# Second attention rebuilt: 32-row tiles for two heads at a time, one ring of three bank pairs, rows spread by DMA

## The reference, cut to what matters

```
q = rope((x @ wq)) -> 32 heads of 8      k = rope((x @ wk)) -> 8 heads of 8      v = (x @ wv) -> 8 heads of 8
scores = einsum('bhqd,bhkd->bhqk', q, repeat(k, 4)) / 8 ** 0.5        # 1024 x 1024, causal
probs  = softmax(where(causal, scores, -inf))
out    = einsum('bhqk,bhkd->bhqd', probs, repeat(v, 4)) -> (2, 1024, 256) @ wo
```

## Time and profile before

| | |
|---|---|
| median of three runs | 2036.06 us |
| the profiled execution's own time | 2036.67 us |
| its span, first to last instruction | 2034.0 us |
| second attention, from the first selection matmul (1169.17) to the end of the last division (1816.9) | 647.7 us |
| its 16 units, counted from one output copy of ACT to the next | 37.5 us for the first, 542.6 for the next 14, 31.2 for the last |

### The profile page before, as it was taken

How to read it: one execution, slowest core, us unless ns; L and a number is a source line. 1 busy time by engine, 2 the same in 40 slices (tenths; PEclk the granted TensorE clock), 3 DMA queues, 4 the chain that set the end, 5 groups by cost and what they waited for, 6 DMA issues and landing times. The chain is left out here.

```text
span 2034.0 us, 46207 instructions
## 1 busy us (share of the span) xinstructions
PE 1759.8 (87%) x15316; PEld 1102.3 (54%) x15316; DVE 1459.2 (72%) x3038; ACT 1157.2 (57%) x2198; POOL 559.5 (28%) x486
## 2 busy tenths in 40 slices
PE   3899999999999999997284789989989999973897
PEld 1577777777777777775142324444444444432455
DVE  4577777777777777776755587778788878825574
ACT  4566666666666666664565325555555555555453
POOL 1555545555545555541311500000000000002011
PEclk9999999999999999999597879999999999986899
DMA  4212211112211111210001000000000000001000
GB/s 127 83 46 50 49 44 47 42 42 49 49 38 47 43 41 47 49 40 3 0 1 64 1 1 1 2 1 0 0 0 0 0 0 0 1 1 62 1 21 21
DMA packets 47508, 56.67 MB, mean 28 GB/s; under 512 B 8337, under 2 KB 29010, under 8 KB 47442
## 3 DMA queue, kind: packets, MB, share of 16 engines
q1 hardware_dynamic: 47442, 55.82, 10.6%
HBM read 20.15 MB, written 2.10 MB: 11 GB/s over the span
## 5 line engine op out<-in xcount | busy, mean ns | idle before, releaser
L1622 ACT ACTIVATE a_prob<-psum 128x768 f32<-128x768 f32 (+5 forms) x384 | 303.7, 810 | 270.3 <-PE psum L1588 146.4
L1658 DVE TENSOR_REDUCE a_mx<-psum 128x1 f32<-128x512 f32 (+3 forms) x608 | 380.7, 659 | 78.0 <-PE psum L1530 48.9
L224 POOL TENSOR_TENSOR x<-x,y (+1 forms) x64 | 54.4, 880 | 980.1 <-ACT y L196 980.1
L1527 PE MATMUL psum<-a_kd,a_qp 128*128 128x512 f16 (+3 forms) x768 | 242.8, 340 | 36.5 <-DVE a_mx L1658 30.0
L1553 PE MATMUL psum<-a_qf,a_kd 128*128 128x512 f16 (+3 forms) x768 | 209.2, 327 | 4.0 <-ACT a_prob L1622 4.0
L528 POOL TENSOR_TENSOR a_swp<-a_swp,a_sin 128x512 f32<-128x512 f32 x128 | 163.4, 1276 | 162.8 <-DMA a_swp<-a_lin 157.9
L1527 PEld LDWEIGHTS psum<-a_kd,a_qp 128*128 128x128 f16 x768 | 73.9, 97 | 226.5 <-DVE a_mx L1658 176.0
L884 DVE TENSOR_REDUCE a_nmax<-psum 128x1 f32<-128x1024 f32 (+7 forms) x256 | 190.8, 746 | 0.6 <-PE psum L599 0.6
L532 POOL TENSOR_TENSOR a_rope<-a_swp,a_cosd 128x512 f32<-128x512 f32 x128 | 164.1, 1282 | 12.4 <-POOL a_swp L528 4.8
L879 DVE TENSOR_TENSOR a_pt_lo_big<-psum,a_pt_hi_big 128x512 f16<-128x512 f32 (+3 forms) x256 | 138.5, 581 | 30.8 <-ACT a_pt_hi_big L751 30.1
L756 ACT ACTIVATE a_prob_big<-psum,a_nmax 128x1024 f32<-128x1024 f32 (+3 forms) x128 | 121.7, 951 | 67.9 <-DVE a_nmax L884 64.6
(11 more groups left out here) (264 smaller groups left out, 4737.4 us busy)
## 6 DMA issues: line engine op xcount, KB each, us to landing
a_swp<-a_lin SPq DMA_DIRECT2D x256, 128.0 KB, 2.3
x<-_attn_hidden_states_dram SPq DMA_DIRECT2D x4, 512.0 KB, 5.5
a_w_raw<-in_L_attn_Wq_dram SPq DMA_DIRECT2D x16, 128.0 KB, 2.2
a_w_raw<-in_L_attn_Wk_dram SPq DMA_DIRECT2D x16, 128.0 KB, 2.3
a_w_raw<-in_L_attn_Wv_dram SPq DMA_DIRECT2D x16, 128.0 KB, 2.2
a_wo_raw<-in_L_attn_Wo_dram SPq DMA_DIRECT2D x1, 2048.0 KB
out_dram<-x SPq DMA_DIRECT2D x4, 512.0 KB, 2.9
f_raw<-in_L_ffn_w_dram SPq DMA_DIRECT2D x2, 704.0 KB, 5.1
```

The lines of the kernel that those rows point to most:

```text
L1527: last = pe.matmul(work(slot, i * n, i * n + n), qp[:, wb, t * P:(t + 1) * P], kd[:, wb, j0 + i, a:e], start=True, stop=not edge)
L1622: act.activation(dst, src, ACT.Exp, scale=SCALE).then_inc(prob_ready, 1)
L1658: dve.tensor_reduce(mx[:, t, j0:j0 + per, p0], work(slot, 0, per * n).rearrange("p (j n) -> p j n", j=per), AX.X, ALU.max).then_inc(work_f ...
```

## The change

What it does:

1. **32-row tiles.** `qp`, `qf` and `kp` hold four heads in four blocks of 32 rows, as before, but no block-diagonal `kd` is made. A QK or KQ matmul now contracts over the 32 rows of one head. Two heads are issued behind one another into the two banks of a pair, each in its own 32 rows of the array.
2. **Rows spread by DMA.** Instead of selection matmuls and copies, SP issues 24 DMAs for each unit (8 rows of 1024 f16 each, L1480 and L1481) that put the rows of queries and keys into place, up to three units ahead. The row that subtracts the maximum is written into `kp` once, ahead of the projections (one `tensor_scalar` over 3 x 1024 columns).
3. **One ring.** All work of a unit, 24 QK jobs (S), 24 KQ jobs (X), 2 turns of maxima (M) and 2 of outputs (O), goes through a ring of three bank pairs in one fixed order, `JOBS`. Job k may start on PE when the reader of job k-3 is done: DVE for S, M and O, ACT for X.
4. **Larger scans.** One DVE instruction takes the maxima of two heads: 24 in place of 38 for each unit.
5. **The causal edge of KQ** is no longer a matmul: GpSimd zeroes it in `prob` after the exponent (`affine_select`, 16 for each unit), and the context waits for it. The mask matmuls of QK stay.
6. **Smaller pieces.** `prob` is two rings (`prob_l` of 2 and `prob_r` of 3 blocks of 512 queries). Values are copied by GpSimd, not ACT. The output leaves in two halves. The code is written out for all 16 units, not looped.

```diff
-        kd = sb("kd", [P, 2, J, S], F16)
-        qp, qf = sb("qp", [P, 2, S], F16), sb("qf", [P, 2, S], F16)
-        kp = sb("kp", [P, 2, BANK], F16)
+        qp, qf, kp = sb("qp", [P, 3, S], F16), sb("qf", [P, 2, S], F16), sb("kp", [P, 3, S], F16)
...
+                    dve.tensor_scalar(kp[:, :, :], kp[:, :, :], minus_row[:, 0:1], None, ALU.add).then_inc(lined, 1)
...
+        def in_order(u):
+            timed = [(i + 0.5, "X", i) for i in range(NJ)] if u >= 0 else []
+            if u + 1 < NU:
+                timed += [(0.87 * i, "S", i) for i in range(NJ)]
+                timed += [(0.87 * (QK.index((3, 0, BANK, 1)) + 1.7), "M", 0), (0.87 * (NJ + 0.7), "M", 1)]
+            if u >= 0:
+                timed += [(19.6, "O", 0)]
+            if u >= 1:
+                timed += [(4.6, "O", 1)]
...
+            def pair_of(k):
+                return (0, 2, 6)[k % 3]
...
+                        for j in range(J):
+                            row = (g * J + j) * HD1
+                            for copy, (q_is, k_is) in enumerate(((0, 0), (0, 1), (1, 0))):
+                                to = slice(j * R + copy * HD1, j * R + (copy + 1) * HD1)
+                                sp.dma_start(qp[to, u % 3, :], q_part[q_is][row % P:row % P + HD1, row // P, tok]).then_inc(loaded_qk[u % 3], 16)
+                                sp.dma_start(kp[to, u % 3, :], k_part[k_is][g * HD1:(g + 1) * HD1, tok]).then_inc(loaded_qk[u % 3], 16)
...
-                                last = pe.matmul(work(slot, i * n, i * n + n), qp[:, wb, t * P:(t + 1) * P],
-                                                 kd[:, wb, j0 + i, a:e], start=True, stop=not edge)
+                        for h in range(2):
+                            rows = slice((2 * pair + h) * R, (2 * pair + h + 1) * R)
+                            last = pe.matmul(c.psum[:, pair_of(k) + h, 0:n], qp[rows, w % 3, t * P:(t + 1) * P],
+                                             kp[rows, w % 3, a:e], start=True, stop=not edge)
...
-                                if n == 0:
-                                    last = pe.matmul(scores[:, 0:P], c.ident_b[:, :], c.mask_kq[:, :], start=False, stop=True)
...
+                    for k, (kind, u, i) in enumerate(JOBS):
+                        slot_free(k)
+                        {"S": scan, "M": maxima, "X": scores, "O": outputs}[kind](k, u, i)
+                        if kind == "X":
+                            done = NJ * u + i - LAG
+                            if done >= 0 and done % 2 == 1:
+                                context(done // NJ, done % NJ // 2)
...
+                                pool.affine_select(out=block_, in_=block_, compare_op=ALU.is_ge, fill=0.0,
+                                                   base=0, pattern=[[0, 2], [1, P]], channel_multiplier=-1).then_inc(masked, 1)
```

More of the change, by code:

```diff
@@ L1426, in attention_1 @@
-        MTS = [("mt", 0), ("mt", 1)]
-        TURNS = [("ot", 0), ("ot", 1)]
-        PREP = KEYS + QS + SCAN + MTS
-        ALL = KEYS + QS + TURNS[:1] + SCAN[:8] + TURNS[1:] + SCAN[8:] + MTS
-        def spread(items):
-            price = [(TB - kt + 1) * len(heads) for kt, heads in STEPS]
-            out, at, total = [], 0, sum(price)
-            for s in range(SUB):
-                upto = -(-len(items) * sum(price[:s + 1]) // total)
-                out.append(items[at:upto])
-                at = upto
-            return out
@@ L1441, in attention_1 @@
-        FIRST_UNIT, ANY_UNIT, LAST_UNIT = spread(PREP), spread(ALL), spread(TURNS)
-        N_FIRST, N_HEAD = 2 * len(PREP) + len(ALL), 2 * len(ALL)
-        assert N_FIRST % 2 == 0 and len(ALL) % 2 == 0
+                QK += [(t, p0 * BANK, min((p0 + 1) * BANK, (t + 1) * P), pair) for pair in range(2)]
+        KQ = []
+        for t in range(TB):
+            for a, e in spans(t * P, S):
+                KQ += [(t, a, e, pair) for pair in range(2)]
+        NJ, NC = len(QK), len(KQ) // 2
+        NU, LAG = B * G1, 3
@@ L1494, in at @@
[L1494 to L1501 removed]
+            rsum = asb("rsum", [P, 2, TB // 2, J])
+            loaded_qk, vg_ready = [sem(f"loaded_qk{i}") for i in range(3)], sem("vg_ready")
+            s_made, scan_done, mcol_ready = sem("s_made"), sem("scan_done"), sem("mcol_ready")
@@ new lines, in maxima, with scores @@
+                    def maxima(k, w, half):
+                        pe.wait_ge(mcol_ready, TB * w + 4 * half + 4)
+                        for i in range(4):
+                            last = pe.matmul(c.psum[:, pair_of(k), i * P:(i + 1) * P], mcol[:, 4 * half + i, :], ident_h[:, :],
+                                             start=True, stop=True)
+                        last.then_inc(m_made, 1)
+                    def scores(k, u, i):
+                        kt, a, e, pair = KQ[i]
+                        pe.wait_ge(qf_ready, 2 * u + a // BANK + 1)
+                        for h in range(2):
+                            rows = slice((2 * pair + h) * R, (2 * pair + h + 1) * R)
+                            last = pe.matmul(c.psum[:, pair_of(k) + h, 0:e - a], kp[rows, u % 3, kt * P:(kt + 1) * P],
+                                             qf[rows, u % 2, a:e], start=True, stop=True)
+                        last.then_inc(x_made, 1)
@@ new lines, in _ @@
+                    for k, (kind, u, i) in enumerate(JOBS):
[5 more added lines that the diff above has]
+                                context(done // NJ, done % NJ // 2)
+                            if u == NU - 1 and i == NJ - 1:
+                                for n in range((NJ - LAG) // 2, NC):
+                                    context(u, n)
@@ new lines, in output @@
+                    def output(u, half):
+                        act.wait_ge(ctx_made, NC * u + (NC if half else last_piece(0, 3, 3 * P)))
+                        wait(act, o_made, 2 * (u - 2) + half + 1)
+                        act.activation(o_sb[:, u % 2, half * BANK:(half + 1) * BANK], c.psum[:, 4 + half, :], ACT.Copy).then_inc(o_ready, 1)
+                    for k, (kind, u, i) in enumerate(JOBS):
+                        if kind == "X":
+                            exponent(k, u, i)
+                            if i == 17:
+                                output(u, 0)
+                            if i == 2 and u >= 1:
+                                output(u - 1, 1)
```

368 lines of the change are left out of this document (131 added, 237 removed).

## The result

| | before | after |
|---|---|---|
| median, lowest and highest of four runs | 2035.93 (2035.03 to 2037.15) | 2068.94 (2064.01 to 2070.67) |
| ratio, 95% interval | | 1.0158 (1.0138 to 1.0178) |
| span of the profiled execution | 2034.0 | 2068.7 |
| mean granted clock over the span | 0.950 | 0.849 |

The forecast was 1985 us, faster. What came is rival R1 in its mixed form, which the prediction priced at 2084 us: the clock of PE is at its half level for part of the time, and more is lost there than the shorter ring wins. One remark on numbers further down: the time of the later kernels differs from run to run, and a ratio to before leaves out runs more than 1.5% above the fastest of their kernel.

The account below looks back on a forecast made before the run. No engine is full; PE and DVE waiting on each other around a small ring bound the kernel. Units -55, start +5, first unit +3, last unit -4 gave -51 from 2036.1: 1985 us, range 1930 to 2130.

Parts of the forecast that it names:

- R1: Rival: PE's clock falls to half level in the attention units, 48.3 us each; all units so, 2185 us; chance 0.31.
- mixed form: Attention units at the half clock for half of the time: 41.6 us per unit, 2084 us in all.
- the sum's clock: Attention units summed at the full clock, 15 x 35.0 us, with 3 us added for a first unit at half clock.
- Ring at the full clock: Chain of PE and DVE through three slots: 12 rounds of 2.42 us plus masks and other jobs, 35.0 us per unit.
- (a): Change between row tiles and full array on PE: taken as 0.11 us; 0 or 0.22 would move a unit by 1.8.
- the term for M and O: Jobs for maxima and outputs in the ring: 3.3 us per unit, between 0 and 5.8.
- (b): Two row tiles on PE run side by side; if not, 0.16 us more per pair, 3.8 per unit.
- R2: Rival: the two row tiles run one behind the other, 38.8 us per unit, no gain there, 2042 us; chance 0.13.
- (c): GpSimd's affine_select of 256 elements: 0.29 to 0.58 us, 16 per unit, hidden, so 0 added.
- (d): SP's 24 DMAs per unit, about 0.5 us each to issue, up to three units ahead: 0 added in the units.
- Start and end: Attention's start 41.3 us against 36.4, so +5; last unit, bound by ACT, 27 against 31.2, so -4.
- R3: Rival: the ring hides other jobs and form changes, 30 to 31.7 us per unit, 1933 us; chance 0.09.

Follow-up runs that it names:

- e3: Changed kernel with each context issued one job later, behind the job that follows its X: 2010.98 us, 0.9904 of before.
- e8: Changed kernel with the causal edge of KQ again a mask matmul on PE and no select on GpSimd: 2068.95 us, 1.0163 of before.
- e1: Changed kernel with every KQ pair of 32-row matmuls issued twice: 2074.77 us, 1.0190 of before.
- e2: Changed kernel with one more 128-row matmul, later overwritten, ahead of every KQ pair: 2043.42 us, 1.0040 of before.

## Why the prediction was wrong, point by point

- **The step that failed** is the sum's clock. It took 15 units at the full clock and charged 3 us for the first alone; R1 got a chance of 0.31. In the profiled execution 66% of the units' time was at the half level (R1's mixed case took 50%), and at 34.3 us for each unit they would have taken 515 us in place of 616: that term was 101 us, not 3. 2070.7 less 101 is 1970, inside the forecast's own range.
- **What should have moved the weight.** The earlier trace rows showed PE at 87% busy in the record and at the half clock. The prediction argued against R1 that a PE nearly full at the half level would be raised again. That is what happens, and then it falls again: PE is busy 93% in 1428 to 1466 at 0.50, and 82% at 1.00 in 1254 to 1275. PE is the fuller one at the low level and the emptier one at the high level. That fits a swing, but how full PE is doesn't settle it alone: in the last unit, which has no scans, PE is busy for 17.82 of 22.3 us, 80%, and before for 23.71 of 31.2, 76%, and both times the clock stays at 1.00. The argument explained the mixed form; it was no argument against the loss. Nor does the row that it names show the rise: the 92% of the earlier trace rows begin at it, and the 3.5 us before, 1203 to 1206.5, have PE busy throughout.
- **Ring at the full clock:** 35.0 forecast, 34.0 to 34.3 measured. Right, with the change of form at 0.10 to 0.11 at both levels. So (a) was right. At the half level 48.3 forecast, 45.7 to 47 measured. That contexts stand in the round was right; e3 put their part at 1.6 to 2.2 us per unit at the full clock. That the term for M and O was right too isn't shown; only the sum was measured.
- **DVE's need:** 26.7 forecast, 26.06 measured; the scan of 1024 columns 1.22 forecast and 1.219 measured.
- **(b) Side by side, R2:** the tiles do run so; R2 is out. By the estimate from the Trainium skill's 3.07 for four row tiles (TensorE: Matmul & The Clock Gate, Part 3) the time would be 18 us later. The trace doesn't bear that out: a pair of 512 columns reaches the next form after 0.32 us, its own stream and the change.
- **(c) `affine_select`:** 0.29 to 0.58 forecast, 0.408 measured, hidden as said (0.7 us of waits in all, under e8).
- **(d) DMA:** issue 0.67 us in place of 0.5, landing 2.0 in place of 2.3: 17.5 us ahead of the first scan, 14.3 forecast. Hidden in the steady units, as said.
- **Start and end:** the scan-only pass took 25.9 us (27 forecast), so the start cost +7.0 against +5. The +3 for a first unit at the half clock belongs to the term that failed. The last unit was ACT's, 22.6 for 27: -8.6 against -4.
- **R3:** out at either level; e3 came nearest, with 32.1 per unit at the full clock.

The Trainium skill (TensorE: Matmul & The Clock Gate, Part 1, "A second HAM failure mode") tells of a kernel that cycles through banks of PSUM, where PE pauses briefly and often between groups of matmuls and swings between its two clocks. The trace agrees: the clock goes between 0.50 and 1.00, with PE waiting 88 us of 400 for DVE's slots. Such pauses are not the whole of it here: the kernel before waited 106.7 us of 400 the same way and stayed at 1.00. The matmuls between the pauses count too, as e1 and e2 show, with 0.79 and 0.92 for the same added stream time.

## What to carry to other kernels

Narrow tiles save PE's time and may give it back through the clock: before you halve the streaming of a kernel in which PE waits inside a ring, price its rounds at the half clock too, and give that case its weight; here PE waited for DVE about as much before and kept the full clock, and the streams between the waits had become shorter and narrower. Read PEclk by stretches before the waits. And take out of the shortest loop whatever needn't stand in it: the same context, one job later, was worth 58 us, by the estimate under e3 most of it through the clock, and more than any of the streams added for the clock's sake.

## What the runs showed of the hardware

- Two matmuls of 32 rows in different row groups run fully side by side, and so do four: from 1454.55 four tiles of 128 columns take 0.22 us until the next form starts, a pair 0.21 (1187.01).
- A change between row tiles and the full array or the column form costs 0.11 us at the half clock (0.54 from a 512-wide pair to the context, 0.43 of it stream) and 0.10 at the full one (0.32, 0.22 of it stream), the same as the column form cost before.
- With the same added stream time (e2's with changes of form besides), PE's clock in the units was 0.79 with 32-row and 0.92 with 128-row matmuls, and 0.67 with neither.
- One unit of the same work took 34.0 us wholly at the full clock and some 47 wholly at the half (changed kernel), by two units read at mean clocks of 0.84 and 0.58.
- One kernel's runs can lie 56 us apart at unchanged instructions, by the clock alone (0.853 to 0.893), where the kernel before, at 0.948 to 0.951, stayed within 5 us.
- A DMA of 8 rows of 2 KB within SBUF takes its queue 0.67 us to issue when one queue issues, and 0.72 to 0.80 when two do.
